# A state-space layer with experts on one core: B and C projected behind the x transposes, and the down product's last 64 rows on two halves of the array

## The reference

```python
zxbcdt = einsum('btd,pd->btp', layernorm(h), W_in)        # z 1024, x 1024, B 64, C 64, dt 16
xBC    = silu(conv4(xBC))                                  # causal, four taps, over x, B and C
dt     = softplus(dt + dt_bias);  dA = exp(-dt * exp(A_log))
state  = state * dA_t + dt_t * B_t * x_t;  y_t = state . C_t + D * x_t
h      = h + rmsnorm(y * silu(z)) * norm_w @ W_out.T
# experts, on layernorm(h): softmax router, top 8 of 32, the weaker four replaced
# by a similar one of the stronger four when the similarity is at least 0.5
h_e    = silu(x @ Wg_e.T) * (x @ Wu_e.T)                   # 192 hidden columns
out    = h + sum_e (h_e * weight_e) @ down_e.T             # 512 columns
```

## Time and profile before

| what | value |
|---|---|
| median of three runs | 1842.42 us (1842.16 to 1848.24) |
| the profiled execution | 1848.1 us, span of the instructions 1846.4 us |
| mean granted TensorE clock | 0.906 of full |
| TensorE matmuls | 1606.8 us busy, 87% of the span |
| VectorE, ScalarE, GpSimd | 52%, 37%, 42% |
| DMA | 195.20 MB, 106 GB/s on average |
| layer, experts | about 410 to 1194 us, about 1207 to 1842 us |

### The profile page before, as it was taken

How to read it: one execution, slowest core, us unless ns; L and a number is a source line. 1 busy time by engine, 2 the same in 40 slices (tenths; PEclk the granted TensorE clock), 3 DMA queues, 4 the chain that set the end, 5 groups by cost and what they waited for, 6 DMA issues and landing times. The chain is left out here.

```text
span 1846.4 us, 29417 instructions
## 1 busy us (share of the span) xinstructions
PE 1606.8 (87%) x8779; PEld 1128.2 (61%) x8780; DVE 953.4 (52%) x2196; ACT 682.7 (37%) x1471; POOL 777.2 (42%) x638
## 2 busy tenths in 40 slices
PE   7999999985799989988989761089999999999996
PEld 7999999954557657574747431055555555555553
DVE  5554545425578986877778554133333333333332
ACT  2525252506487583745547210022222222222221
POOL 4220200011224264757464657545455554545454
PEclk9999999987799997979889675589999999999998
DMA  7110000015244344333413110177777776776665
GB/s 271 61 58 1 12 1 12 2 58 197 78 109 147 91 120 117 89 100 89 143 40 99 36 22 15 30 197 175 157 157 181 157 173 160 163 180 166 157 114 92
DMA packets 96680, 195.20 MB, mean 106 GB/s; under 512 B 38392, under 2 KB 46880, under 8 KB 91857
## 3 DMA queue, kind: packets, MB, share of 16 engines
q0 software_dynamic: 36992, 88.26, 22.2%
q1 hardware_dynamic: 59600, 105.78, 19.3%
HBM read 144.15 MB, written 49.84 MB: 105 GB/s over the span
## 5 line engine op out<-in xcount | busy, mean ns | idle before, releaser
L1868 PE MATMUL moe_ps_gu<-moe_wgu,moe_xt 128*128 x960 | 333.2, 490 | 0.0
L1742 POOL DMA_INDIRECT out_h<-moe_yy,moe_idx_s x121 | 190.9, 1578 | 274.9 <-DVE moe_idx_s L1797 138.1
L1015 POOL DMA_INDIRECT scratch_slots<-lay_toki,lay_slot x192 | 215.9, 1124 | 59.0 <-issue 58.2
L1868 PEld LDWEIGHTS moe_ps_gu<-moe_wgu,moe_xt 128*128 128x128 f32 x960 | 173.7, 191 | 98.0 <-issue 1.7
L1852 PE MATMUL moe_ps_y<-moe_wd,moe_ht 96*128 x484 | 228.8, 595 | 3.4 <-DVE moe_ht L1823 3.1
L1780 ACT ACTIVATE moe_sl<-moe_ps_gu 128x192 f32<-128x192 f32 x120 | 39.7, 331 | 443.7 <-PE moe_ps_gu L1868 318.4
L1196 PE MATMUL lay_ring<-lay_xnt,win_sb 128*128 128x128 f32 (+2 forms) x1152 | 173.2, 299 | 23.4 <-ACT lay_xnt L1096 18.1
L1196 PEld LDWEIGHTS lay_ring<-lay_xnt,win_sb 128*128 128x128 f32 (+2 forms) x1152 | 155.2, 203 | 32.9 <-ACT lay_xnt L1096 18.8
L1412 DVE SCALAR_TENSOR_TENSOR lay_xa<-lay_ring,head_cw,lay_xa 128x378 f32<-128x378 f32 (+5 forms) x240 | 142.4, 609 | 58.6 <-ACT lay_xa L1067 52.6
L1280 PE MATMUL lay_ring<-head_wout,lay_yb 128*128 128x512 f32 x384 | 171.3, 600 | 0.0
L1736 POOL DMA_INDIRECT moe_xg<-scratch_xg,moe_idx_g x123 | 131.1, 1066 | 47.4 <-issue 22.1
(11 more groups left out here) (284 smaller groups left out, 2744.9 us busy)
## 6 DMA issues: line engine op xcount, KB each, us to landing
lay_m<-scratch_cum SPq DMA_DIRECT2D x16, 1536.0 KB
moe_wgu<-in_wgu SPq DMA_DIRECT2D x32, 768.0 KB
moe_wd<-in_wd SPq DMA_DIRECT2D x32, 384.0 KB
out_h<-lay_hres SPq DMA_DIRECT2D x48, 128.0 KB
scratch_xg<-lay_x SPq DMA_DIRECT2D x48, 128.0 KB
win_sb<-in_win SPq DMA_DIRECT2D x1, 4384.0 KB, 15.9
tok_u_raw<-in_tok_u SPq DMA_DIRECT2D x16, 256.0 KB, 4.0
tok_v_raw<-in_tok_v SPq DMA_DIRECT2D x16, 256.0 KB, 4.9
```

The source lines that it names most:

```text
L1015: pool.indirect_dma_start(out=a["slots"], out_offset=bass.IndirectOffsetOnAxis(ap=slot[:, j, k:k + 1], axis=0), in_=toki[:, j:j + 1], in_o ...
L1742: pool.indirect_dma_start(out=a["out"], out_offset=bass.IndirectOffsetOnAxis(ap=idx_s[n][:, 0:1], axis=0), in_=yy[n][:], in_offset=None, b ...
L1868: last = mm(ps_gu[b][:], xt[b][:, t], wgu[:, bass.ds(r * KD + t, 1)].rearrange("p o n -> p (o n)"), start=t == 0, stop=t == KD - 1)
```

## The change

In the layer, both B (with dt) and C of pair n + 1 are projected behind the x transposes of pair n, the ring's order follows, ScalarE takes both first taps between dt's size and its exp, VectorE convolves both behind all six x_dt and ahead of the b=1 state matrix, and that matrix is made in two instructions of eight heads with a signal each, on which the state products wait separately.

In the experts, the down weights lie as 128 rows by three blocks of 256 columns: the first 128 hidden rows for the left and for the right half of the output, and a third block with the last 64 hidden rows, left half of the output on partitions 0 to 63, right half on 64 to 127 (the same 384 KB). VectorE writes the last 64 hidden columns twice, in a second instruction; so their transposition has them on both halves of the partitions. ScalarE copies the third block of the entry's weights to a buffer of its own. `down` is then two matmuls over 128 rows and two over 64, the one on rows 0 to 63 and the other on rows 64 to 127 of the array, into two banks.

```diff
 def ring_order():
-    order = [("bc", 0, 0)]
+    order = [("bc", 0, 0), ("bc", 0, 1)]
...
-        if n + 1 < PAIRS:
-            order.append(("bc", n + 1, 0))
         if n < PAIRS:
             order += [("xt", n, k) for k in range(N_XT)]
+        if n + 1 < PAIRS:
+            order += [("bc", n + 1, 0), ("bc", n + 1, 1)]
...
-                def steps_in(i):
+                def projected_bc(i):
                     src = halves("bc", i, 0)[NS:NS + NH]
                     nc.scalar.activation(dtr[:], src, ACT.Identity, bias=dtb[:]).then_inc(dtr_done, 1)
-                    own.step(nc.scalar.activation(dtn[:], src, ACT.Abs, bias=dtb[:]))
+                    size = own.mark(nc.scalar.activation(dtn[:], src, ACT.Abs, bias=dtb[:]))
+                    first_tap(i, "bc", 0, TB)
+                    first_tap(i, "bc", 1, TC)
+                    own.wait(size)
                     own.step(nc.scalar.activation(dtn[:], dtn[:], ACT.Exp, scale=-1.0))
...
-                        pe.wait_ge(m_done, i * 2 + 1)
+                        pe.wait_ge(m_done, i * 3 + 1)
...
-                    if pairs(i):
-                        pe.wait_ge(m_done, i * 2 + 2)
                     for m2 in range(4):
                         if pairs(i):
+                            pe.wait_ge(m_done, i * 3 + 2 + m2 // 2)
                             state_products(i, 1, m2)
...
-                    if pairs(n + 1):
-                        project_b(n + 1)
                     if pairs(n):
                         for k in range(N_XT):
                             x_transposes(n, k)
+                    if pairs(n + 1):
+                        project_bc(n + 1)
...
-                    v.scalar_tensor_tensor(m0[:, b], m0[:, b], 1.0, gm[:, b].unsqueeze(1).to_broadcast([P, NH, SEQ]),
-                                           ALU.min, ALU.mult).then_inc(m_done, 1)
+                    for h0, h1 in ((0, NH),) if b == 0 else ((0, NH // 2), (NH // 2, NH)):
+                        v.scalar_tensor_tensor(m0[:, b, h0:h1], m0[:, b, h0:h1], 1.0,
+                                               gm[:, b].unsqueeze(1).to_broadcast([P, h1 - h0, SEQ]),
+                                               ALU.min, ALU.mult).then_inc(m_done, 1)
...
                         if pairs(n):
                             x_dt(n, k)
-                        if k == 2 and pairs(n + 1):
-                            conv(n + 1, 0)
...
+                    if pairs(n + 1):
+                        conv(n + 1, 0)
+                        conv(n + 1, 1)
                     if pairs(n):
                         state_matrix(n, 1)
...
+                        r = entry(act, F_RING, i * STEPS + n + 1, W_RING - 1)
+                        nc.scalar.copy(wdr[b][:], wd[:, bass.ds(r * 3 + 2, 1)].rearrange("p o n -> p (o n)")).then_inc(rest_act, 1)
...
-                        v.scalar_tensor_tensor(hh[b][:], sl[b][:], cwv[b][:], ps_gu[b][:, FF:2 * FF],
+                        v.scalar_tensor_tensor(hh[b][:, 0:P], sl[b][:, 0:P], cwv[b][:], ps_gu[b][:, FF:FF + P],
+                                               ALU.mult, ALU.mult)
+
+                        v.scalar_tensor_tensor(hh[b][:, P:2 * P].rearrange("p (o n) -> p o n", o=2),
+                                               sl[b][:, P:FF].unsqueeze(1).to_broadcast([P, 2, FR]), cwv[b][:],
+                                               ps_gu[b][:, FF + P:2 * FF].unsqueeze(1).to_broadcast([P, 2, FR]),
                                                ALU.mult, ALU.mult).then_inc(h_dve, 1)
...
-                def down(r, ht_count):
+                def down(r, n, ht_count):
                     pe.wait_ge(ht_dve, ht_count)
+                    pe.wait_ge(rest_act, ht_count)
                     for q in range(2):
-                        last = mm(ps_y[:], ht[:, q], wd[:, bass.ds(r * 2 + q, 1)].rearrange("p o n -> p (o n)"), start=q == 0, stop=q == 1)
+                        mm(ps_y[:, q, 0:DH], ht[:, 0], wd[:, bass.ds(r * 3 + q, 1)].rearrange("p o n -> p (o n)"), start=True, stop=False)
+                    for q in range(2):
+                        k = slice(q * FR, (q + 1) * FR)
+                        last = mm(ps_y[:, q, 0:DH], ht[k, 1], wdr[n][k], start=False, stop=True)
                     last.then_inc(down_pe, 1)
```

More of the change, by code:

```diff
@@ L698 @@
 FF = 192
-FH = FF // 2
+FR = FF - P
+DH = D // 2
 ENTRIES = 256
@@ L710, in ring_order @@
 def ring_order():
-    order = [("bc", 0, 0)]
+    order = [("bc", 0, 0), ("bc", 0, 1)]
     for i in range(-1, PAIRS + 1):
         n = i + 1
-        if n < PAIRS:
-            order.append(("bc", n, 1))
         if 0 <= i < PAIRS:
@@ L1117, in _ @@
                 rows_in(0)
-                steps_in(0)
-                first_tap(0, "bc", 0, TB)
+                projected_bc(0)
                 for i in range(-1, PAIRS + 1):
@@ L1307, in x_transposes, with project_bc @@
                     last.then_inc(ring_pe, 1)
-                def project_b(i):
+                def project_bc(i):
                     pe.wait_ge(xnt_done, i + 1)
-                    project(i, "bc", 0, *BC_TILES[0][:2])
+                    for k in range(2):
+                        project(i, "bc", k, *BC_TILES[k][:2])
                 token_rows(0)
-                project_b(0)
+                project_bc(0)
                 for i in range(-1, PAIRS + 1):
                     n, r, w = i + 1, i - 1, i - 2
-                    if pairs(n):
-                        project(n, "bc", 1, *BC_TILES[1][:2])
                     if pairs(i):
-                        pe.wait_ge(m_done, i * 2 + 1)
+                        pe.wait_ge(m_done, i * 3 + 1)
                         pe.wait_ge(xdt_done, i * N_XT + N_XT)
@@ L1664, in build_experts @@
         wgu = s.sb("wgu", [P, W_RING * KD, 2 * FF])
-        wd = s.sb("wd", [FH, W_RING * 2, D])
+        wd = s.sb("wd", [P, W_RING * 3, DH])
+        wdr = [s.sb(f"wdr{n}", [P, DH]) for n in range(2)]
         xg = [s.sb(f"xg{n}", [P, XW]) for n in range(STEPS)]
@@ L1668, in build_experts @@
         sl = [s.sb(f"sl{n}", [P, FF]) for n in range(2)]
-        hh = [s.sb(f"hh{n}", [P, FF]) for n in range(2)]
-        ht = s.sb("ht", [FH, 2, P])
+        hh = [s.sb(f"hh{n}", [P, 2 * P]) for n in range(2)]
+        ht = s.sb("ht", [P, 2, P])
         yy = [s.sb(f"yy{n}", [P, D]) for n in range(2)]
@@ L1677, in build_experts @@
         ps_xt = s.bank("ps_xt", [P, KD, P])
-        ps_y = s.bank("ps_y", [P, D])
+        ps_y = s.bank("ps_y", [P, 2, D])
         ps_ht = s.bank("ps_ht", [P, 2, P])
@@ L1696, in build_experts @@
         sl_act = s.sem("sl_act")
+        rest_act = s.sem("rest_act")
         h_dve = s.sem("h_dve")
@@ L1775, in _ @@
                 nc.scalar.copy(xt[0][:], ps_xt[:]).then_inc(xt_act, 1)
+                act.wait_ge(rest_act, 1)
                 with act.Fori(0, iters_r) as i:
@@ L1788, in _ @@
                 v.memset(hh[1][:], 0.0).then_inc(h_dve, 1)
+                v.memset(wdr[1][:], 0.0).then_inc(rest_act, 1)
                 dve.wait_ge(tab_in, 16)
@@ L1876, in _ @@
                         last.then_inc(t_pe, 1)
-                        down(r_down, i * STEPS + n + 1)
+                        down(r_down, 1 - b, i * STEPS + n + 1)
                 r_down = entry(pe, F_RING, iters_r * STEPS, W_RING - 1)
                 hidden(1, iters_r * STEPS + 1)
-                down(r_down, iters_r * STEPS + 1)
+                down(r_down, 1, iters_r * STEPS + 1)
 INPUTS = ("tok_u", "tok_v", "tok_b", "tok_c", "tok_ldt", "win", "cat", "wout", "nw", "gate", "cw", "cb", "dcol",
@@ L1934 @@
         cb[:NS, m] = conv_b[c0:c0 + NS]
+    w_down = x["L0_ffn_down_proj"].transpose(0, 2, 1).reshape(E, FF, 2, DH)
+    wd = np.zeros((E, P, 3, DH), w_down.dtype)
+    wd[:, :, 0:2] = w_down[:, 0:P]
+    for q in range(2):
+        wd[:, q * FR:(q + 1) * FR, 2] = w_down[:, P:FF, q]
     arrays = {
@@ L1952 @@
         "wgu": x["L0_ffn_gate_up_proj"].reshape(E, 2 * FF, KD, P).transpose(0, 3, 2, 1),
-        "wd": x["L0_ffn_down_proj"].reshape(E, D, 2, FH).transpose(0, 3, 2, 1),
+        "wd": wd,
     }
```

21 lines of the change are left out of this document (9 added, 12 removed).

## The result

The kernel after takes **1774.99 us** (median of four runs, 1770.32 to 1780.81), the kernel before 1842.29: a ratio of 0.962, 95% interval 0.9583 to 0.9657. That is 67 us, against 25 forecast, and outside the range. The profiled execution took 1780.8 (span 1779.1).

The account below looks back on a forecast made before the run. Bound in the layer's batch turns: list-scatter batch end, then remaining routing and state products; in the experts: TensorE or scatters. Gains 18 + 3 + 1 + 3 = 25 us from 1842.4 give 1817, range 1803 to 1854.

Parts of the forecast that it names:

- State products earlier: Layer, TensorE: first state product of the 767 us turn starts at 770.2 in place of 774.05, 3.9 us early.
- Turns without a batch: Layer turns without fourteen list scatters beside the state products: less VectorE idling, 3 us in the first, 1 in two following.
- Turns with a batch: Layer turns beside GpSimd's fourteen list scatters: first routing signal passes inside the batch, 4.5 us each, four turns, 18 us.
- 10.2 if two turns escape: Layer, turns with a batch: upper bound per turn, should two routing turns pass before the batch ends; 4.5 was taken.
- The experts: Expert loop: cheaper down less the cost of the split hidden product, net 3 us (bounds 5 slower, 17 faster).
- The down: Experts' down product: 1.64 us against 1.72, row halves together plus 0.35 for shape changes; 0.08 saved per down.
- 64 entries: Experts: the chain goes through the down in about 64 of 121 entries, by scatters on the others; 64 x 0.08 = 5 us.
- the split hidden product: Experts, VectorE: hidden product in two instructions takes 0.28 us more, costing about 2 us where it counts.
- (a): Layer: first routing turn's signal is caught as before, batch end stays the gate, layer gains 4, 1835 us; chance 0.22.
- (b): Experts: row halves don't run together, down 2.07 us, 0.35 more, near 1854 us, slower; chance 0.12.
- (c): Layer: TensorE's clock falls in front of the state products, which then run slower, 1862 us; chance 0.10.
- (d): Experts: row halves switch for free, down 1.29 us, experts gain some 17 us, 1803 us; chance 0.07.

Follow-up runs that it names:

- one_half: The kernel after with both products of the last 64 rows on rows 0 to 63 of the array, not on separate halves: 1817.03 us in one run.
- after_whole: The kernel after with the b=1 state matrix made in one instruction again: 1796.55 us, ratio to before 0.9755.
- the shorter batch: List scatters in shares 5, 5, 4, 10 in place of 3, 3, 4, 14; on the second chip before so changed 1778.9 us, after 1756.35.
- held_before: The kernel before with GpSimd held behind the batch's third scatter until the turn's third routing block is turned: 1855.26 us, ratio 1.0047.

## Why the prediction was wrong

**State products earlier.** Foreseen 3.9 us against the norm, measured 3.7 (7.5 to 3.8). Right.

**Turns without a batch.** Foreseen 3 + 1 = 4, measured twice that. The first pair's turn, for which 3 was meant, gained 3.8 (in the other two pairs of profiles of before and after 6.9 and 3.3), though not as foreseen: VectorE does all six x_dt first, but its idle of the earlier trace rows did not go away. It now waits 6.08 us for the tap, which comes later on ScalarE, in place of 3.90:

```profile
479.00 3.69 DVE L1411 SCALAR_TENSOR_TENSOR lay_xa<-lay_ring,head_cw,lay_xa 64x382 f32<-64x382 f32 x6 [6.08 <-ACT lay_xa L1068]
```

TensorE, whose first state product starts at 474.3 in place of 481.7, waits 2.20 and 0.90 us behind that, and its products then run at half clock (0.91 us per record from 480.95 on, 0.55 before it). The two turns that follow gained 3.9 + 0.3 where 1 was foreseen: in the first the whole earlier start of the state products passed through, in the second next to nothing of it.

**Turns with a batch: the step that failed.** The prediction says: the first turn's signal passes, "when the batch ends, TensorE has the third turn next", 4.5 us per turn, four turns, 18. Measured 9.3 + 13.2 + 6.7 + 12.7 = 41.9. The mechanism was right: state products 3.8 us earlier within the batch, the first copy at 766.3, 12.2 us into it. But I took from the earlier trace rows that everything behind the first turn falls to the batch's end. In after, the second copies come 14.4 to 18.6 us into batches of 21.8 to 22.3 us, in three of four turns at most 0.8 us late. The bound "10.2 if two turns escape" was in the text and was priced as an edge. Three things were missing. First, what stands over when the batch ends was 14.4 to 15.2 us in all four turns of before and is 0 to 7.0 after, and the forecast subtracted 5.1 from it once. Second, in before TensorE itself crawls in the late phase. Its fifth state product, in the trace of before:

```profile
782.01 0.38 PE L1212 MATMUL lay_ring<-lay_m,lay_xdt 128*64 128x192 f32 x1
782.99 0.55 PE L1212 MATMUL lay_ring<-lay_m,lay_xdt 128*64 128x192 f32 x3 [0.59 <-issue]
...
787.29 0.36 PE L1215 MATMUL lay_ring<-lay_m,lay_xdt 64*64 64x64 f32 x2 [0.68 <-issue]
788.70 0.26 PE L1215 MATMUL lay_ring<-lay_m,lay_xdt 64*64 64x64 f32 x1 [1.05 <-issue]
```

That is 6.9 us for a product of 1.48, and I had not read it. Third, with it goes the half clock: the forecast kept the remainder at 2.50 us per product, but in after the one from 769.04 to 770.51 takes 1.47. In turn 5 the clock falls at 835.8, and this is the turn that gains least, 6.7.

**The last turn** got nothing in the forecast, since it has no B; its 3.1 us were missed.

**The experts.** Foreseen 3 us, measured 17 in the trace, 11 with the part alone (interval 7 to 16). The down: 1.64 foreseen, 1.59 measured. Two shape changes cost 0.30 beyond the passes and not 0.35, and the pair holds. The step that was missed on that side is the wider transposes of the hidden block, 0.05 more, so that 4.887 per entry is the forecast's 4.88 by two errors that cancel. What failed is the factor: I counted 64 entries from the chain's 6% of 1846 us. The chain view follows one path, and where it goes round by scatters it does not show that TensorE is as close. At 0.072 us on 119 intervals the saving is 8.6. The 2 us for the split hidden product are not seen. The rest is long entries: beyond its usual length the loop of before has 25 to 29 us in three profiles, that of after 20, 23 and 28. So of the other 8 us of the trace a good part is chance: over the seven traces with the old experts the loop takes 616.4 us on average and over the twelve with the new ones 603.9, a difference of 12.4 (one_half left out).

**Rivals.** (a) fell: the first signal passes in turns 3 to 6 of all three profiles of after. (b) fell: 0.43 us per entry is what one_half measures without the pair. (c) fell as named, in the turn shown the clock stays full from 753 to 774; but it was half true: the clock does fall in the first pair's turn, and with a wait of 1.6 us among the state products after_whole loses 22 us, and 0.50 stands there. (d) was out by 0.30 us per down, and the layer, not the down, brought the time below 1803. The Trainium skill (TensorE: Matmul & The Clock Gate, Part 3) gives the span of packed tiles as one matmul and about 4 ns for each further one. The two halves agree, they start 6 to 7 ns apart; but the span has no term for the change of shape, and here that costs the 0.30 us.

**What stays open.** By which way the scatters hold up TensorE's signals, and why the second chip doesn't show it with the same scatters in the same places. The first copy is late in before at 14.5 us into the batch and the second is not in turn 5 of after at 17.7, so time since the batch's start alone doesn't decide it. Why no first copy of the last pair is let through (in after it is 5.2 us late, 1.9 behind the batch) is open too. Nor was there a profile of before itself on the second and fifth chips, and no run took work off VectorE.

## To carry to other kernels

A gain that hangs on a late signal should be worked out for each consumer behind it and not only for the first: here one shift of 3.8 us let through one, two or three turns of the routing, and was worth 7 to 13 us. Cost what comes back as well: in the two traces without late signals and with the shorter batch the same shift is worth nothing, as VectorE is busy for 67 of 71.4 us of a turn either way, and a batch that is held back takes its late signals along to the z products. And take the number of entries that an engine bounds from the spread of the loop's periods, not from one chain.

## What the hardware showed beyond that

- **Chips differ.** The same before took 1842 to 1849 us on four chips and 1787 on one, where TensorE's signals were on time throughout.
- **GpSimd's list scatters and TensorE's signals.** On one kind of chip, copies up to 8.2 us late (782.1 to 790.3, before) and a silu 12.1 us late (held_before) with scatters beside them, at most 0.15 without; the wait ends some 2 us behind the last scatter.
- **VectorE against GpSimd.** A VectorE product of 0.94 us took 3.95 beside a gate of 3.44; a scatter of 0.98 took 3.99 beside one 3.35 us instruction, and 4.66 in after beside two halves in a row.
- **Row halves.** Two products on rows 0 to 63 and 64 to 127 run fully together; the changes of shape cost 0.30 us per down, as 1.59 is six spans of 0.215 and 0.30. By the starts, 0.09 of it stands in front of the first half-row record, 0.10 between the first two passes of these, and 0.10 in front of the transposes.
